# Mixing stage of a vision tower: shared down product from two fp32r parts with the rests on GpSimd, and slots by choice

## What is computed

```python
h = attention(x) @ w_out.T + b_out                  # 8 x 512 x 256; a class token is put ahead
h = h + state_mix(layernorm(h))                     # circulant recurrence, kept as a scan between two rotations
u2 = layernorm(h)
shared = silu(u2 @ Wg_s.T) * (u2 @ Wu_s.T) @ Wd_s.T # inner width 512
scores, idx = top_k(sigmoid(u2 @ Wr.T + rb), 2)     # 8 experts, two per token
out = shared + sum over e of weight_e * expert_e(u2)
h = h + out
```

## Time and profile before

| | |
|---|---|
| median of 3 runs | 1162.68 us (1161.87 to 1164.88) |
| the profiled execution, its own time | 1163.81 us |
| its span, first to last instruction | 1161.9 us |
| mean granted TensorE clock | 0.987 of full speed |
| busy: PE, DVE, ACT, POOL | 96%, 79%, 50%, 34% of the span |
| one middle batch of the mixing stage | 34.94 us |

### The profile page before, as it was taken

The page is one execution under the profiler, slowest core; times in us unless marked ns, Lnnn a source line. Parts: engine busy times, 40 slices in busy tenths (PEclk is TensorE's granted clock), DMA queues, the critical chain, the costliest instruction groups (busy, mean ns, idle before and its releaser), DMA issues.

```text
span 1161.9 us, 22261 instructions
## 1 busy us (share of the span) xinstructions
PE 1116.7 (96%) x6090; PEld 718.5 (62%) x6091; DVE 916.8 (79%) x1571; ACT 584.2 (50%) x973; POOL 394.3 (34%) x508
## 2 busy tenths in 40 slices
PE   9999999999999999989999999969999999999996
PEld 5654333333333333477777787757888888888885
DVE  4788888888888887678888888777777777777774
ACT  4445777777777777631233222432444444444442
POOL 2002621011111101214345443353555555554553
PEclk9998999999999999989999999999999999999998
DMA  7887333332333322041244541122333333333332
GB/s 232 273 273 259 92 89 88 93 99 81 95 85 90 103 72 87 1 164 42 68 109 109 100 98 39 38 47 78 55 55 54 51 56 52 51 53 54 54 55 32
DMA packets 109714, 105.37 MB, mean 91 GB/s; under 512 B 42464, under 2 KB 97904, under 8 KB 109648
## 3 DMA queue, kind: packets, MB, share of 16 engines
q1 hardware_dynamic: 92704, 85.38, 26.2%
q0 software_dynamic: 16960, 19.38, 10.5%
HBM read 64.88 MB, written 39.68 MB: 90 GB/s over the span
## 4 chain that ended last, share of the span: by engine, by line
PE 73%; DVE 10%; issue 3%; POOL 3%; ACT 1%; another core or an unknown queue 0%; DMA 0%; POOLq 0%; DVEq 0%; ACTq 0%
PE mix_pairs L73 20%; PE pv L688 11%; PE by_key L675 10%; PE by_query L666 9%; PE mix_made L1874 9%; PE mix_turn L1861 3%; POOL kept_table L1130 3%; PE mix_made L1282 2%; PE mix_made L1270 2%; PE by_query L709 2%; PE mix_turn L1841 1%; PE mix_pairs L1308 1%; PE mix_made L1253 1%; DVE mix_stats L1462 1%; DVE k_mix_u L1472 1%
## 5 line engine op out<-in xcount | busy, mean ns | idle before, releaser
L762 DVE TENSOR_REDUCE k_neg_max<-by_query 128x2 f32<-128x1024 f32 x240 | 282.8, 1220 | 48.4 <-PE by_query L666 45.2
L823 ACT ACTIVATE k_wu_e<-by_key 128x512 f32<-128x512 f32 x512 | 270.1, 600 | 64.9 <-PE by_key L675 64.8
L675 PE MATMUL by_key<-k_wg_e 99*128 99x512 bf16 x512 | 175.1, 384 | 2.8 <-PEq L147 2.4
L1818 POOL DMA_INDIRECT out_rows<-x_y,k_slot x72 | 114.0, 1583 | 156.1 <-PE mix_turn L1841 104.6
L666 PE MATMUL by_query<-k_wg_e 96*128 96x512 bf16 x480 | 144.7, 382 | 0.0
L1918 ACT ACTIVATE x_gate<-mix_pairs 128x512 f32<-128x512 f32 x72 | 43.0, 597 | 196.8 <-PE mix_pairs L73 196.8
L688 PE MATMUL pv<-k_wu_e,k_wd_e 128*17 128x512 f32 x1024 | 134.5, 598 | 0.3 <-ACT k_wu_e L823 0.3
L73 PE MATMUL mix_pairs<-w_short,x_T 128*128 x288 | 120.8, 419 | 2.2 <-issue 2.2
L1874 PEld LDWEIGHTS mix_made<-x_wd,x_acts_T 128*128 128x128 f32 x864 | 111.2, 188 | 7.4 <-ACT x_acts_T L1941 0.9
L73 PE MATMUL mix_pairs<-w_short,x_rest 128*128 x288 | 113.9, 396 | 0.0
L1874 PE MATMUL mix_made<-x_wd,x_acts_T 128*128 128x256 f32 x864 | 112.6, 279 | 0.7 <-ACT x_acts_T L1941 0.7
(11 more groups left out here) (251 smaller groups left out, 1960.8 us busy)
## 6 DMA issues: line engine op xcount, KB each, us to landing
k_wg_e<-kept_qk SPq DMA_DIRECT2D x384, 64.0 KB, 2.3
kept_qk<-k_qk_parts SPq DMA_DIRECT2D x32, 384.0 KB, 3.4
kept_v<-k_v_ones SPq DMA_DIRECT2D x8, 544.0 KB, 5.3
k_wd_e<-kept_v SPq DMA_DIRECT2D x32, 136.0 KB, 2.7
k_wu_e<-in_xT SPq DMA_DIRECT2D x8, 512.0 KB, 4.6
kept_heads<-k_wd_e SPq DMA_DIRECT2D x8, 512.0 KB, 3.0
k_heads_in<-kept_heads SPq DMA_DIRECT2D x8, 512.0 KB
k_wg_e<-in_wg_e SPq DMA_DIRECT2D x8, 512.0 KB, 4.7
```

The costliest lines, as they stand in the source:

```text
L675: pe.matmul(by_key[:, key_bank(job), :], k_rows[0:SROWS, g, h, kt * P:(kt + 1) * P], q_rows[0:SROWS, g, h, :], start=True, stop=True).then ...
L762: dve.tensor_reduce(neg_max[:, g % 2, 2 * n:2 * n + 2], by_query[:, bank:bank + 2, :], AX.X, ALU.max, negate=True).then_inc(query_read, 1)
L823: act.activation(probs[:, key_tile(j) // 2 * G + j // 2 % G, j % 2, :], by_key[:, key_bank(job), :], ACT.Exp, scale=float(HD) ** -0.5).the ...
L1818: pool.indirect_dma_start(out=dram["out"], in_=y[:, r % 2, :], in_offset=None, compute_op=ALU.add, out_offset=bass.IndirectOffsetOnAxis(ap ...
```

## The change

It has two parts that touch the same stretch of a step.

First, the shared down product of batches 0 to 6 is made of two fp32r parts. wd_s is cut once, in step 0, into `wd_s_short` (ACT) and `wd_s_rest` (DVE). In each step ACT makes `gate_short` from the shared expert's inner activations in two halves (`shorten_acts`), and POOL subtracts it, again in two halves, into `gate_rest`, which lies in the place of `gate` (`rest_of_acts`). POOL does this after it has waited for both halves of the state. PE does 16 short products of each of the two halves and then 16 products of the rests (`shared_down_parts`). The last batch (7) keeps the fp32 product.

Second, `place` is called once for each choice. The first choice's slots stand where both stood, the second choice's behind `shared_add`. POOL scatters the four tiles of choice 0 first and then the four of choice 1; the power of the next batch still stands behind six scatters.

To make room in SBUF, wd_e is loaded early for two experts only; the four in between are loaded in step 7 (`load_late("down_made", ...)`), and the semaphore counts are fitted to that. Some class-token semaphores are merged into `cls_products`; that moves no instruction.

```diff
@@ slots
-def slot_rows(dve, link, mem, t, row_id, par):
+def slot_rows(dve, link, mem, t, row_id, par, choices=range(2)):
-    for n in range(2):
+    for n in choices:
...
+EARLY_DOWN = 2
@@ SP
-                for name in ("wg_e", "wu_e", "wd_e") if e < E - 2 else ("wg_e", "wu_e"):
+                for name in ("wg_e", "wu_e", "wd_e") if e < EARLY_DOWN else ("wg_e", "wu_e"):
...
+                if this and not nxt:
+
+                    load_late("down_made", 2 * b, range(EARLY_DOWN, E - 2))
...
-                    load_late()
+                    load_late("gate_made", FC * B, (E - 2, E - 1))
@@ POOL
+            def rest_of_acts(j, half):
+                pool.wait_ge(ev["acts_shortened"], 2 * j + half + 1)
+                some = slice(2 * half, 2 * half + 2)
+                pool.tensor_tensor(short(gate_rest[:, some, :]), gate[:, some, :], gate_short[:, some, :],
+                                   ALU.subtract).then_inc(ev["acts_cut"], 1)
...
+                    if prev:
+
+                        pool.wait_ge(ev["state_done"], DC * (b + 1))
+                        rest_of_acts(b - 1, 0)
+                        rest_of_acts(b - 1, 1)
                     inverse_deviation(b, 2)
...
-                    pool.wait_ge(ev["slots_ready"], b)
-                    pool.sem_inc(mem["dma_begun"])
-                    for t in range(TT):
-                        if t == TT - 1 and nxt:
-                            inverse_deviation(b + 1, 1)
-                            pool.sem_inc(mem["dma_begun"])
-                        for n in range(2):
+                    for n in range(2):
+                        pool.wait_ge(ev["slots_ready"], 2 * (b - 1) + n + 1)
+                        pool.sem_inc(mem["dma_begun"])
+                        for t in range(TT):
+                            if n == 1 and t == TT - 2 and nxt:
+                                inverse_deviation(b + 1, 1)
+                                pool.sem_inc(mem["dma_begun"])
@@ ACT
+            def shorten_acts(j, half):
+                act.wait_ge(ev["act_done"], FC * j + 2 * half + 2)
+                act.wait_ge(ev["down_made"], 2 * j)
+                some = slice(2 * half, 2 * half + 2)
+                act.activation(short(gate_short[:, some, :]), gate[:, some, :], ACT.Copy).then_inc(ev["acts_shortened"], 1)
...
-                    act.wait_ge(mem["experts_in"], 16 * (3 * (E - 3) - 2))
+                    act.wait_ge(mem["experts_in"], 16 * 2 * (E - 3))
...
+                if this and prev:
+                    shorten_acts(b - 1, 0)
                 if prev:
                     silu(b - 1, 2)
...
                     silu(b - 1, 3)
+                if this and prev:
+                    shorten_acts(b - 1, 1)
...
             act.activation(cls_gate, cls_ps[1].rearrange("p (m n) -> p m n", m=FC), ACT.Silu).then_inc(ev["cls_silu"], 1)
+            act.activation(short(wd_s_parts[0][:, :, :]), mem["wd_s"][:, :, :], ACT.Copy).then_inc(ev["shared_shortened"], 1)
@@ PE
+            def shared_down_parts(j):
...
+                pe.wait_ge(ev["act_done"], FC * j + FC - 1)
+                if j == 0:
+                    pe.wait_ge(ev["w_s_cut"], 3)
+                for part, groups in ((0, (0, 1)), (0, (2, 3)), (1, range(FC))):
+                    if part == 0:
+                        pe.wait_ge(ev["acts_shortened"], 2 * j + groups[1] // 2 + 1)
+                    else:
+                        pe.wait_ge(ev["acts_cut"], 2 * j + 2)
+                    for t in range(TT):
+                        for m in groups:
+                            for n in range(2 - part):
+                                mm = pe.matmul(pairs[:, 0, t // 2, (t % 2) * D:(t % 2 + 1) * D],
+                                               short((gate_short, gate_rest)[part][:, m, t * P:(t + 1) * P]),
+                                               short(wd_s_parts[n][:, m, :]),
...
-                if prev:
+                if this and prev:
+                    shared_down_parts(b - 1)
+                elif prev:
                     shared_down(b - 1, 0)
                     shared_down(b - 1, 1)
@@ DVE
+                if not prev:
+                    dve.wait_ge(ev["shared_shortened"], 3)
+                    dve.wait_ge(mem["heads_stored"], 16 * B)
+                    dve.tensor_tensor(short(wd_s_parts[1][:, :, :]), mem["wd_s"][:, :, :], wd_s_parts[0][:, :, :],
+                                      ALU.subtract).then_inc(ev["w_s_cut"], 1)
...
                 elif nxt:
-                    place(b - 1, 1 - par)
+                    place(b - 1, 1 - par, 0)
...
+                if prev and nxt:
+
+                    place(b - 1, 1 - par, 1)
```

84 lines of the change are left out of this document (49 added, 35 removed).

## The result

| chip of | kernel before | changed kernel | ratio (95% interval) |
|---|---|---|---|
| the first pair | 1162.28 us (6 runs) | 1155.99 us (6) | 0.9943 (0.9924 to 0.9963) |
| e5 to e8 | 1160.08 us (28) | 1157.66 us (12), e6 | 0.9978 (0.9967 to 0.9989) |
| e9 to e12 | 1159.53 us (25) | 1156.73 us (12), e9 | 0.9978 (0.9964 to 0.9992) |
| e5 to e8, a second time | 1158.69 us (23) | 1155.65 us (12), e17 | 0.9969 (0.9956 to 0.9983) |

What follows compares the result with a forecast made beforehand. Two almost equal chains meeting at POOL's power were taken to set the 34.94 us batch. Terms -6.4 + 0.9 + 0.4 = -5.1 us gave 1156.8 from the 1161.9 span, 1157.6 carried to the median; range 1155.9 to 1161.2.

Steps and rivals of the forecast that it cites:

- the costs at the end: Batch 7 and the tail: one more slot conversion each on VectorE, 0.2 us each, 0.4 us in all.
- rival 4: TensorE's clock falls in batch 7 behind a longer wait, costing some 1.5 us: 1159.1 us; no chance of its own.
- Down product: Shared down product on PE, seven batches: 5.60 us instead of 6.91, saving 1.31 us each.
- ScalarE's copies and the rests: Middle batches: ScalarE's two 1.02 us copies hidden; POOL's two rests, 2.38 us each, do not move the power.
- rivals 1 and 2: POOL's rests end late: 0.9 us late together, 1163.1 us (0.10); both at 3.26 us, 1168.5 us (0.10, shared with end costs).
- no cover is left: POOL's rests use up the time before the power; each further 0.1 us moves the power by 0.1.
- Slots and two chains: Middle batches 1 to 6: both chains meeting at POOL's power shorten by 1.07 us a batch, 6.4 us in all.
- Rival 3: Only one of the two chains gets short: 0.5 to 0.7 us a batch, 1160.4 us; chance 0.12.
- (start) +0.9: Batch 0: DVE's cut of wd_s delays the turn of u2, 0.9 us lost once; bounds 0.1 to 1.3.
- (end) +0.4: The same term as the costs at the end: two extra slot conversions, 0.2 us each.
- The clock in batch 1: Within rival 4: a clock that holds in batch 1 would give 1.5 us back, 1156.1 us.
- the four late loads of wd_e: Loads moved to batch 7, on SP's queue: cost zero, unless they are 20 us late.

Runs made afterwards that it cites:

- e5: The kernel before, run again with no edit on the chip of e6: 1159.71 us.
- e8: Changed kernel with e7's edits, second choice's slots behind the next batch's first sum, four scatters instead of six ahead of GpSimd's power: 1155.29 us, 0.9959.
- e6: The changed kernel run again with no edit, on the chip of e5: 1157.66 us, 0.9978 of the kernel before.
- e9: The changed kernel a third time, no edit, on another chip: 1156.73 us, 0.9978 of the kernel before.
- e12: Changed kernel with the two rests made on VectorE, ahead of its last sum and statistics, instead of GpSimd: 1177.05 us, 1.0150 of the kernel before.
- e17: The changed kernel a fourth time, no edit, on the chip of e5 to e8: 1155.65 us, 0.9969 of the kernel before.
- e4: Changed kernel with a third operation of the rests' size on GpSimd, for which the down product waits: 1170.12 us, 1.0098 of the kernel before.
- e1: Changed kernel with both choices' slots made before the normalising again, so only the down product is new: 1164.33 us, 1.0048 of the kernel before.
- e2: Changed kernel with the fp32 shared down product back and no rests, slots still choice by choice: 1162.15 us, 1.0027 of the kernel before.
- e7: Changed kernel with batch 0's weight cut behind the normalising, one slot conversion in the last two batches, five unread products in batch 7: 1157.07 us, 0.9975.
- e14: Kernel before with only eight unread products in batch 1's wait ahead of its y product: 1160.80 us, 0.9994 of the kernel before.
- e15: Changed kernel with only eight unread products in batch 1's wait ahead of its y product: 1156.52 us, 0.9946 of the kernel before.
- e18: The kernel before a third time, no edit, on the same chip as e17: 1157.96 us, 0.9993.
- e3: Changed kernel without GpSimd's rests and their product, 32 down steps instead of 48: 1158.03 us, 0.9991 of the kernel before.
- e13: Changed kernel with only five unread products in batch 7, behind the router's products: 1155.84 us, 0.9953 of the kernel before.

## Why the prediction was right and where it was wrong

**The step that failed is the costs at the end.** I had put them at +0.4 us, for two more conversions on VectorE, and had left TensorE's clock in batch 7 out of the sum, as rival 4. The runs showed 1.6 to 2.5 us there in each profile of the changed kernel, nearly all of it the clock; the conversion of batch 7 cost 0.06 (the other was not measured by itself). The direction and the mechanism of the middle batches were right: two chains that end together, both shortened. That the first chip's 6.3 us lies near my 5.1, on its other side, is luck at least in part; the three repetitions gained 2.4 to 3.0.

- **Down product.** 5.60 us forecast, 5.92 measured; from the y product's start to the turn of u2 1.17 us saved of 1.31. A product took 0.12 us in place of 0.1167. The difference lay in slack and cost nothing.
- **ScalarE's copies and the rests.** Hidden, as said: 2.37 us a rest (2.38 taken), power not moved. The power started 4.88 us behind the start of the rests, released by VectorE's statistics; the rests had taken 4.73 us of these (4.9 forecast), so rivals 1 and 2 fell; e4 shows that the next 2.36 us cost 2.1 a batch, which was the claim that no cover is left.
- **Slots and two chains.** 1.07 us a batch forecast. Measured 1.02 in batch 1 (39.90 against 38.88, both at full clock) and 4.83 over the five periods behind it, 0.97 each: 5.85 of 6.4 us. The last of the five gave 0.8 only. Rival 3 had 0.5 to 0.7 a batch and falls; e1 and e2 show that one chain alone gives nothing.
- **(start) +0.9.** 0.90 between the same two rows where the clock holds (e5, e1, e7; e17 has 0.89). Where it falls in 490 to 495 us, PE's products there last longer and the late cut is hidden: 17.73 us in e14 with the kernel before, 17.75 in e15 with the changed one, on the same chip. In three of four profiles of the changed kernel the clock fell there, so the stretch as a whole was 1.64 us longer than before; and the attention ends up to 2 us sooner or later by its own clock.
- **(end) +0.4: the step that failed.** The conversions are there, and cost less than said: the cut of u2 in batch 7 starts 28.42 us behind the turn of u, 28.36 before. The clock belonged in the sum: it fell in every profile of the changed kernel and in none of the three of the kernel before. The wait grew from 0.54 to 1.39 us (1.8 forecast, for the turn of u2 came 0.8 us sooner and not 1.1); the price of 1.5 was low (1.6 to 2.5), and I gave the fall no chance of its own. The fall is not the change's alone, for in e14 it came behind 0.53 us of waiting.
- **The range** doesn't follow from its own terms. The clock kept in batch 1 and the start at its lower bound give 1157.6 - 1.5 - 0.8 = 1155.3, and rival 3 with the clock's cost 1160.4 + 1.5 = 1161.9, where I wrote 1155.9 and 1161.2.
- **The clock in batch 1** comes and goes with both kernels: half clock in all three profiles of the kernel before, in two of four of the changed one.

The sum with measured terms: -1.02 - 4.83 + 0.90 + 1.6 to 2.5 = -3.4 to -2.5 us, and the medians of the repetitions gave -2.4 to -3.0. Single profiles scatter far more: the spans of e6 and e5 differ by 5.2 us, those of e17 and e18 by 1.0. On the first chip they differ by 8.4: beyond these terms (-3.35), 1.47 is the clock of batch 1, 2.3 the last column of the table (37.8 against 35.5), 0.5 the experts' stage (360.5 against 360.0), and the start shows 0.1 in place of 0.9. The attention ended 1.57 us earlier after the change, in which its half-clock stretch near 105 us was missing; the half clock beside the class token's products, and the late cut with it, took 1.64 back. In e9 the stretch near 105 us and the one in batch 1 were at half clock again, and the one beside the class token's products too. That the medians of six runs carried the same luck is argued from the profiles, not shown.

Still open: the waits of ScalarE in the last batch, why the slot load into the experts took from 7.8 us (e5) to 10.7 (e7), and what lets the clock fall behind 0.53 us of waiting once and not another time. Nor did a run put the four late loads of wd_e back: that they cost nothing, as I said, is not shown, for the last column varies too much.

## What to carry to other kernels

Where two chains end within 0.1 us of each other, a change to one of them is worth nothing or less, and only both together pay. An operation can stand better on the engine that waits, even at twice its duration, as long as it ends before that engine is needed: here two operations of 2.37 us fitted and a third did not. A saving on TensorE that turns into waiting can be taken back by its clock: count that as a term of the sum wherever a wait grows, and repeat the profile before reading a few microseconds out of one.

## What the runs showed of the hardware

- Granted clock and waits: 1.39 us of idle time ahead of the last up products was followed by half clock (1.2 GHz) in five of five profiles of the changed kernel without the five products, and in e1, e3 and e4; 0.53 us at the same place was in one of four; 2.8 to 3.1 us in batch 1 in five of seven of the two plain kernels. Five products that nobody reads, put into the first of these waits, kept the clock up in six of six. The Trainium skill, TensorE: Matmul & The Clock Gate, section "HAM oscillation — how this bites in real kernels", tells of such falls behind waits for DMA. These rows agree that idle time goes ahead of the falls, and show one behind as little as 0.53 us.
- GpSimd's two rests ran at 2.37 us each while VectorE did sums from PSUM; its add, beside VectorE's cut of two SBUF operands, took 3.26 us here too.
- The same kernel's median differs by chip and call: over six sets of runs, one of each row of the first table and those beside e1 and e13, the kernel before took 1158.7 to 1162.3 us, and the changed one over four 1155.7 to 1157.7.
